# How many graphs get their shared expert during attention, and how many beside the final sums: 8 and 6 against 11 and 3

## The reference, cut to what matters

```python
x = x + gcn3(layernorm(x), adj)                 # three graph convolutions
x = x + moe_8_experts_top2(layernorm(x))
x = x + attention(layernorm(x), adj)            # 8 heads, tanh(adj * scores)
x = x + moe_64_experts_top2_with_shared(layernorm(x))
```

```python
h = silu(buf @ w1) * (buf @ w3);  y = h @ w2          # per expert, on gathered rows
routed = (y_pairs * top_scores).sum(axis=1)
shared = silu(xf @ sw1) * (xf @ sw3) @ sw2            # every token, hidden width 256
return shared + routed
```

## Time and profile before

| what | value |
|---|---|
| median of 3 runs | 2153.25 us (2152.39 to 2153.28) |
| the profiled execution's own time | 2144.97 us |
| its span, first to last instruction | 2142.9 us |
| granted TensorE clock, mean | 0.964 |
| PE busy | 1896.0 us (88%) |
| DVE busy | 1481.8 us (69%) |
| ACT busy | 1231.0 us (57%) |
| POOL busy | 1055.3 us (49%) |
| DMA moved | 311.54 MB, mean 145 GB/s |

### The profile page before, as it was taken

The page is one execution under the profiler, slowest core; times in us unless marked ns, Lnnn a source line. Parts: engine busy times, 40 slices in busy tenths (PEclk is TensorE's granted clock), DMA queues, the critical chain, the costliest instruction groups (busy, mean ns, idle before and its releaser), DMA issues. The chain is left out here.

```text
span 2142.9 us, 37719 instructions
## 1 busy us (share of the span) xinstructions
PE 1896.0 (88%) x12098; PEld 1422.8 (66%) x12098; DVE 1481.8 (69%) x3275; ACT 1231.0 (57%) x1870; POOL 1055.3 (49%) x1246
## 2 busy tenths in 40 slices
PE   7999999983898999997899999989886888887886
PEld 6989988882888888885345444444434766666753
DVE  5777777853666666664798889899984555554559
ACT  4444444421666666664787888877762555555630
POOL 3355555533333333335566675677433455565630
PEclk9999999986999999998899999999997999998999
DMA  7444445114555545553423213223211654444559
GB/s 299 149 177 174 176 178 188 40 41 149 180 173 188 186 168 178 176 194 135 148 80 122 88 63 123 73 91 125 70 36 62 194 161 133 139 132 113 150 210 354
DMA packets 136790, 311.54 MB, mean 145 GB/s; under 512 B 36030, under 2 KB 66976, under 8 KB 132576
## 3 DMA queue, kind: packets, MB, share of 16 engines
q1 hardware_dynamic: 106144, 267.69, 37.3%
q0 software_dynamic: 30528, 42.37, 5.8%
HBM read 202.59 MB, written 147.56 MB: 163 GB/s over the span
## 5 line engine op out<-in xcount | busy, mean ns | idle before, releaser
L1864 ACT ACTIVATE c_att<-c_att 128x1024 f32<-128x1024 f32 x256 | 268.7, 1056 | 126.9 <-DVE c_att L2047 118.5
L2047 DVE TENSOR_TENSOR c_att<-c_p_s,adj 128x1024 f32<-128x1024 f32 x256 | 300.4, 1215 | 57.2 <-PE c_p_s L1588 53.9
L2409 POOL DMA_INDIRECT moe_y<-adj,d_goal x236 | 237.8, 1007 | 185.3 <-ACT adj L2371 114.9
L1153 POOL DMA_INDIRECT moe_y<-b_y,b_goal x144 | 163.3, 1134 | 317.5 <-DVE b_y L1210 281.5
L221 PE MATMUL b_p_y<-b_w2h,b_hh 128*128 128x256 f32 x576 | 168.9, 293 | 9.5 <-DVE b_hl L227 7.4
L629 POOL DMA_INDIRECT moe_in<-a_xn,a_rows x128 | 141.5, 1105 | 57.6 <-issue 32.5
L222 PE MATMUL b_p_y<-b_w2l,b_hh 128*128 128x256 f32 x576 | 160.8, 279 | 0.0
L223 PE MATMUL b_p_y<-b_w2h,b_hl 128*128 128x256 f32 x576 | 160.8, 279 | 0.0
L227 DVE TENSOR_TENSOR b_hl<-b_ht,b_hh 128x512 fp32r<-128x512 f32 (+1 forms) x160 | 101.5, 638 | 78.8 <-ACT b_ht L1352 76.0
L1545 POOL DMA_INDIRECT moe_in<-c_xn,c_rows x128 | 131.0, 1024 | 50.0 <-issue 36.6
L1601 PE MATMUL c_p_o<-c_att,c_xp 128*32 128x512 f32 x1024 | 140.6, 622 | 6.3 <-ACT c_att L1864 3.9
(11 more groups left out here) (290 smaller groups left out, 5656.3 us busy)
## 6 DMA issues: line engine op xcount, KB each, us to landing
b_w<-in_moe_w SPq DMA_DIRECT2D x80, 512.0 KB
moe_in<-b_zeros SPq DMA_DIRECT2D x65, 520.0 KB, 10.8
adj<-in_adj SPq DMA_DIRECT2D x32, 1024.0 KB, 6.2
d_xin<-moe_in SPq DMA_DIRECT2D x38, 520.0 KB
b_xin<-moe_in SPq DMA_DIRECT2D x32, 520.0 KB, 5.6
c_g<-moe_y SPq DMA_DIRECT2D x32, 512.0 KB
moe_y<-c_zeros SPq DMA_DIRECT2D x32, 512.0 KB
d_w<-in_moe_w SPq DMA_DIRECT2D x64, 256.0 KB
```

The costliest lines, as they stand in the source:

```text
L1153: pool.indirect_dma_start(out=m["moe0_y"], out_offset=bass.IndirectOffsetOnAxis(ap=goal[:, h, t:t + 1], axis=0), in_=y[:, h, t, :], in_off ...
L1864: act.activation(part, part, ACT.Tanh).then_inc(att_ready, 1)
L2047: dve.tensor_tensor(att[:, u % 2, 2 * c:2 * c + 2, :], p_s[:, 2 * c:2 * c + 2, :], adj[:, h, u % T, :].unsqueeze(1).broadcast_to([P, 2, N] ...
L2409: pool.indirect_dma_start(out=m["moe1_y"], out_offset=bass.IndirectOffsetOnAxis(ap=goal[0:n, j, t:t + 1], axis=0), in_=y[0:n, j, t, :], in ...
```

## The change

Three graphs (8, 9 and 10) move from `LATER` to the ones that get their shared expert in attention. `LATER` goes from six graphs (8 to 13) to three (11 to 13), and everything that is worked out from it follows: `going_up`, `going_down`, `keep_busy`, the stores and loads of `later_xt`, `ORDER` and the loops over `NLATER`.

```diff
-OWN = 8
+OWN = 11
 LATER = tuple(range(OWN, B - 2))
```

## The result

| | before | after |
|---|---|---|
| median | 2152.23 us (20 runs, 2148.72 to 2162.59) | 2158.79 us (20 runs, 2151.08 to 2166.63) |
| profiled execution's span | 2142.9 us | 2157.0 us |
| ratio | | 1.0028, 95% interval 1.0017 to 1.0039 |

The kernel became slower by 0.28%: 6.0 us of 2152, with 3.7 to 8.4 us as the interval. (The ratio is an estimate from all runs and not the quotient of the medians; these are 6.6 us apart.) The forecast was +6.9 us (2160.2 us, 0.32%).

The account below looks back on a forecast made before the run. The prediction took PE to bound attention graphs with a shared expert, and DMA, with VectorE also full, the final sums. +7.4 us in attention and -0.5 us in the sums gave +6.9 us, 2160.2 us, range 2155.5 to 2163.0.

Parts of the forecast that it names:

- Attention, +7.4 us: Attention loop: three more graphs with the shared expert, each 2.46 us longer, add 7.4 us.
- keep_busy as 4.3 us of PE: Attention graphs without the shared expert: keep_busy's multiplications take 4.3 us of PE per graph, which moved graphs lose.
- Ahead of the sums, zero: Between experts and first sum: three 512 KB loads fewer, 4 us of DMA time, hidden by POOL; no change.
- The sums, -0.5 us: Final sums: VectorE loses 7.2 us of work but waits 0.8 us per graph on DMA; only 0.5 us comes back.
- A: Final sums: VectorE bounds them, so all 7.2 us come back, 2153.5 us, no change; chance 0.12, whole or half.
- B: Experts' stage: the clock falls elsewhere, up to 2.5 us either way; chance 0.14 of over 1.5 us.
- C: Attention, graphs 8 to 10: the shared expert costs half, sum +3.2 us, 2156.4 us; chance 0.03.

Follow-up runs that it names:

- e_nobusy8: The kernel before with keep_busy doing nothing in graphs 8 to 13: 2079.63 us against 2069.83, ratio 1.0048.
- e_own12: The kernel before with 12 graphs' shared expert in attention and 2 beside the sums: 2075.88 us against 2068.61, ratio 1.0031.
- e_half8: The kernel before with the sums' second result load left out from the fourth graph on: 2066.55 us, ratio 0.9986.
- e_own12b: The 12-and-2 split again from the same source, on another chip, against the kernel before: 2078.00 us against 2069.33, ratio 1.0040.
- e_tanh11: The changed kernel with tanh in place of silu in attention's shared expert: 2074.71 us, ratio 1.0023 against the kernel before.
- e_own11: The changed kernel run again, beside the kernel before: 2074.55 us against 2068.61, ratio 1.0024.

## Why the prediction was right

**Attention, +7.4 us: right.** The loop grew by 7.2 us in the first pair of profiles and by 7.4 to 7.5 us in the later ones (489.0, 488.9 against 496.4). The working was right too, not only the difference of two windows: with PE's work cut by 3.4 us the period falls by 2.0 us at once and stops near the free graphs' 36.1; with ACT's table loads removed it stays. The Trainium skill's drain of about 1380 ns with each switch of tables (ScalarE: Activation LUTs, "What ACT_TABLE_LOAD costs") did not show: in the trace before, the instruction behind a table load starts where the load ends (1310.67 + 1.28, the next at 1311.96), ACT's busy time fell by 2.7 us for two loads less, which is 2 x 1283 ns and some tenths, and the period did not move. No run here had ACT as the bound of a graph, so what such a drain would cost there is not shown.

**keep_busy as 4.3 us of PE: right** (32.32 to 28.01 us in e_nobusy8). What it does besides, holding up the clock, was not in the sum and did not need to be, as the last graphs keep theirs in both kernels.

**Ahead of the sums, zero: right.** From VectorE's last instruction of the experts to its first gate it is 5.4 us before and 5.5 us after, and from there to the first sum 14.3 to 14.4 us in the profile of every kernel here, with seven, six, three or two loads of later_xt.

**The sums, -0.5 us: the mechanism right, the bound too tight.** DMA does hold the changed kernel's sums, and VectorE's 7.2 us turned into waits of 0.73 us per graph (8.1 us over eleven), where 0.8 had been said. But I took 411 GB/s as the best rate that the engines could have, and stayed near the lower end "because the share of 1.02 to 1.03 over 30 us leaves no room". There was room: 419 GB/s at the same share. The term is not one number but depends on the execution's course: +0.3 us in the first pair, and down to -3.5 us (56.3 against 59.8 us) with 12 graphs. That the forecast's -0.5 us lies near the mean of them is in part luck. Over these profiles the kernels with all loads and 8 graphs took 59.6, 59.8 and 62.2 us, those with 11 took 57.5 to 62.0 us with a mean of 59.7 us over six; that is about 0.8 us back, with a spread as large as itself.

**The sum.** +7.4 - 0.5 = +6.9 us was forecast. The three measurements of the change are 1.0028, 1.0024 and 1.0026, which is +6.0, +5.0 and +5.4 us. All lie a little under what the loop alone says, as does e_own12 (+6.4 and +8.3 us by ratio, where the loop says +10.1). An even DMA course in some of the executions, which only the kernels with few later graphs can use, would do that; since only profiled executions show their course, it is argued and not shown. A rival is left: in the twelve later profiles the experts' stage, whose code the change does not touch, took 332.8 to 337.2 us (mean 334.2) with 11 or 12 graphs in attention and 333.6 to 339.5 us (mean 336.4) with 7 or 8, and the stretch behind the loop was about 1 us shorter with 12. Single profiles that spread so widely do not decide it, and in the first pair the experts differ the other way. The intervals (1.0009 to 1.0039 at the widest) hold the forecast as well.

**The rivals.** A (VectorE bounds the sums) fell in its full form: no 7.2 us came back. It may be right in a part: at 419 GB/s the sums of the kernel before would have VectorE as their bound, at 58.3 us. That is an estimate from e_half8 and e_own12; no profile with all loads and eight graphs had that rate. The Trainium skill's figure of about 425 GB/s for a core alone (HBM Reference, Specifications), which I had set aside for the trace's 411, is near the 419 of the even course. B (the clock falls elsewhere) had as its sign a change of over 1.5 us in the experts, and the first pair shows one, 2.1 us. But the sign was too fine: the changed kernel alone gave 333.0 and 334.9 us in two profiles, and the mean granted clock of the stage was 0.95 in both kernels of the first pair. So B is neither shown nor needed. Behind the loop the stretch was 104.5 to 106.3 us in all kernels that keep keep_busy. The 4.3 us ahead of attention between the first two profiles I had not priced. C (attention takes the work for less) is out: three periods of 38.5 to 38.9 us.

No version that does the same computation came out below the kernel before. Seven graphs in attention is level with eight, and more is slower.

## What to carry to other kernels

Moving work from one stage to another is a trade at two marginal prices, and both are read where the engine in question is full. Here 2.46 us a graph were paid in attention, because PE was full there, and nearly nothing came back at the end, because VectorE and DMA were full at once and only VectorE was relieved. When two engines finish within a few per cent of one another (here 58.3 of 59.8 us), count the gain of relieving one as the distance to the other, and then ask what the other's own spread is: a DMA busy share of 1.0 went with 380 as well as with 419 GB/s here, so it is no sign of the best rate. A pair of single profiles says nothing of a change of 0.3% as a whole; the stretch that the change touches can be read to a few tenths, if it is compute-bound.

## What the runs showed that I had not expected

The DMA engines moved the same pattern of loads and stores at 419 GB/s in one execution (e_own12) and at 369 to 394 in another of the same kernel on another chip (e_own12b), with a busy share of 1.03 and 0.99 to 1.02. On one chip the same two courses stood in kernels that differ only in a function in attention: 419 in two windows of e_tanh11, 358 to 390 in e_own11.

The experts' stage took 413 and 415 us in the first two profiles, and 333 to 340 us in all twelve later ones, the kernel before (335.5 us) and the changed one (333.0 and 334.9 us) among them, from the same source. The gate products of successive experts (L2471) show it: in the first two profiles their distance over the first thirty experts alternates between 5.35 and mostly 8.7 to 8.8 us, in the later ones it is 5.34 us each time. What made every second expert wait some 3.4 us there was not found, and neither was whether it lies in the chip or in the occasion. It does not touch the comparison, since both kernels had it or neither.

Taking away multiplications whose result nobody reads made the kernel 10 us slower: in the graphs without them the granted clock fell to 0.50 for a time (a mean of 0.95 in four of five windows).
